# A window-attention block with a routed mixture of experts: the score bias copied into the score banks by ScalarE, with a new order of work on every queue

## What is computed

```python
attn = jnp.einsum('whnd,whmd->whnm', q, k) * scale + bias[None]     # 8x8 windows, 4 heads
attn = jax.nn.softmax(attn, axis=-1)
out = jnp.einsum('whnm,whmd->whnd', attn, v)
...
x = x + _L0_conv_ref(_ln_c(x), ...)        # windowed attention on channel-normalised x
t = t + _L0_ffn_ref(_ln_t(t), ...)         # per token: top 2 of 8 experts, 64x64 each, gated
```

## Time and profile before

| | |
|---|---|
| median of 3 runs | 1152.08 us (1149.42 to 1155.35) |
| profiled execution, span | 1154.0 us |
| TensorE busy | 1050.4 us (91%), mean granted clock 0.985 |
| VectorE busy | 875.0 us (76%) |
| ScalarE busy | 748.4 us (65%) |
| GpSimd busy | 463.1 us (40%) |
| transfers | 189.61 MB, 164 GB/s |

### The profile page before, as it was taken

The page is one execution under the profiler, slowest core; times in us unless marked ns, Lnnn a source line. Parts: engine busy times, 40 slices in busy tenths (PEclk is TensorE's granted clock), DMA queues, the critical chain, the costliest instruction groups (busy, mean ns, idle before and its releaser), DMA issues.

```text
span 1154.0 us, 39247 instructions
## 1 busy us (share of the span) xinstructions
PE 1050.4 (91%) x16886; PEld 597.6 (52%) x16886; DVE 875.0 (76%) x1355; ACT 748.4 (65%) x1218; POOL 463.1 (40%) x509
## 2 busy tenths in 40 slices
PE   4798899999999999999999999999999999988857
PEld 3455555555555555555555544555555555554312
DVE  4567678878777777787777877778887787787874
ACT  1688577767776767677766666777776677665410
POOL 1013443444344334434434443443434434443550
PEclk9999999999999999999999999999999999999878
DMA  6016467878777668877776787677778876747885
GB/s 188 2 39 138 106 148 173 202 184 193 177 168 170 171 166 192 194 172 170 181 168 166 187 187 181 155 177 180 177 176 193 195 172 164 171 112 178 190 179 130
DMA packets 48872, 189.61 MB, mean 164 GB/s; under 512 B 10494, under 2 KB 10750, under 8 KB 32572
## 3 DMA queue, kind: packets, MB, share of 16 engines
q1 hardware_dynamic: 48700, 187.10, 68.3%
HBM read 151.15 MB, written 18.87 MB: 147 GB/s over the span
## 4 chain that ended last, share of the span: by engine, by line
PE 59%; DVE 19%; POOL 7%; DMA 6%; issue 6%; ACT 2%; SPq 0%; POOLq 0%; DVEq 0%; ACTq 0%
PE bank L568 8%; PE bank L689 8%; PE bank L585 8%; PE bank L546 5%; PE bank L559 5%; DMA gz<-gates_dram 5%; DVE Ls L1827 5%; PE bank L602 4%; PE bank L609 4%; DVE probs L1728 3%; DVE mx L1721 3%; PE bank L621 3%; PE bank L516 3%; POOL vr L1527 3%; PE bank L630 2%
## 5 line engine op out<-in xcount | busy, mean ns | idle before, releaser
L689 PE MATMUL bank<-gz,wex 64*64 64x512 f32 x2048 | 259.4, 612 | 9.0 <-DVE gz L1743 9.0
L1536 POOL TENSOR_TENSOR gz<-gz,tt 128x1024 f32<-128x1024 f32 x94 | 229.2, 2440 | 63.9 <-DMA gz<-gates_dram 63.9
L1117 ACT ACTIVATE pt<-bank 128x512 f32<-128x512 f32 x256 | 151.7, 593 | 119.7 <-PE bank L585 118.8
L1728 DVE TENSOR_TENSOR probs<-bank,mx 128x1024 f32<-128x1024 f32 x128 | 156.7, 1224 | 94.7 <-PE bank L585 91.6
L1743 DVE TENSOR_TENSOR gz<-gz,tt 128x1024 f32<-128x1024 f32 x156 | 196.9, 1280 | 5.0 <-DMA gz<-gates_dram 5.0
L1497 POOL TENSOR_TENSOR tt<-prj,xs 128x512 f32<-128x512 f32 x64 | 82.4, 1308 | 291.3 <-ACT prj L1134 291.3
L1721 DVE TENSOR_REDUCE mx<-bank 128x16 f32<-128x1024 f32 x128 | 156.0, 1219 | 34.4 <-PE bank L568 33.5
L585 PE MATMUL bank<-cst,probs 128*128 128x128 f32 x1024 | 165.7, 285 | 3.0 <-ACT pt L1117 2.5
L585 PEld LDWEIGHTS bank<-cst,probs 128*128 128x128 f32 x1024 | 111.7, 141 | 87.8 <-issue 67.5
L568 PE MATMUL bank<-km,qs 32*64 32x128 f32 x4096 | 143.8, 275 | 4.8 <-issue 4.8
L689 PEld LDWEIGHTS bank<-gz,wex 64*64 64x64 f32 x2048 | 74.2, 135 | 125.6 <-issue 104.2
(11 more groups left out here) (122 smaller groups left out, 1480.0 us busy)
## 6 DMA issues: line engine op xcount, KB each, us to landing
gz<-gates_dram SPq DMA_DIRECT2D x250, 512.0 KB, 8.7
xs<-in_x SPq DMA_DIRECT2D x32, 512.0 KB, 9.0
tx<-tt SPq DMA_DIRECT2D x128, 128.0 KB, 2.8
out<-ob SPq DMA_DIRECT2D x128, 128.0 KB, 9.9
gz<-in_rel SPq DMA_DIRECT2D x1, 2048.0 KB, 9.5
gates_dram<-gt_rs SPq DMA_DIRECT2D x32, 64.0 KB
cst<-in_consts SPq DMA_DIRECT2D x1, 359.0 KB, 3.0
tt<-in_weights SPq DMA_DIRECT2D x4, 64.0 KB, 5.0
```

What stands on the lines that cost most here:

```text
L689: last = mm(bank[64 * x:64 * x + 64, Y_BANK + a, :], wex[64 * a:64 * a + 64, e, :], gz[64 * a:64 * a + 64, s.pair(e)[1], e % 2, x * CH:(x ...
L1117: af(pt[g % 2][:, u % 2, :, :, :, :].rearrange("p j h x q -> p (j h x q)"), bank[:, PT_BANK, :], ACT.Copy).then_inc(pt_ready, 1)
L1536: tt_(gz[:, k, e % 2, :], gz[:, k, e % 2, :], tt[s.buf(4)][:, :], op=ALU.mult).then_inc(z_pool, 1)
L1728: tt_(probs[g % 2][:, :, :, :].rearrange("p h w (m k) -> p (h w m) k", k=N), two_banks(S_BANK).rearrange("p (c k) -> p c k", k=N), mx[g % ...
```

## The change

Bias products on TensorE are replaced by a copy on ScalarE, `put_bias`, one per score group: it writes `bias` (float32, now a tile of its own), repeated over windows, into both score banks once `shift` has read the group before; `scores` waits for it and adds all its products on top. `tile_id` and `bias_hl` and the operations that made them are dropped. `open_scores` runs one product per score bank at the start, so that later products add onto what lies in the bank. `bias_rows` gathers into the expert banks instead of the score banks.

```diff
             def scores(s, g):
                 if g == 0:
                     pe.wait_ge(q_ready, s.count(1, 1))
                     pe.wait_ge(k_ready, s.count(2, 2))
-                    if s.c == 0:
-                        pe.wait_ge(bias_ready, 1)
-                wait(pe, shift_done, s.count(GROUPS, g))
-                for hp in range(2):
-                    mm(bank[:, S_BANK + hp, :], tile_id[:, :],
-                       bias_hl[:, 2 * hp:2 * hp + 2, :].rearrange("p h k -> p (h k)").unsqueeze(1).broadcast_to(
-                           [P, 4, 2 * N]), start=True, stop=False, skip_group_check=True)
-
+                pe.wait_ge(bias_put, s.count(GROUPS, g + 1))
...
+            def open_scores():
+                for hp in range(2):
+                    last = mm(bank[:, S_BANK + hp, :], cv("ident"), cst[:, 0:512], start=True, stop=True)
+                last.then_inc(scores_open, 1)
...
+            def put_bias(s, g):
+                if s.c == 0 and g == 0:
+                    act.wait_ge(scores_open, 1)
+                    act.wait_ge(bias_part, 6)
+                wait(act, shift_done, s.count(GROUPS, g))
+                af(two_banks(S_BANK).rearrange("p (h i k) -> p h i k", h=2, k=2 * N),
...
+                   ACT.Copy).then_inc(bias_put, 1)
```

More of the change, by code:

```diff
@@ L387, in _ @@
             spread_gates(strips[0], 3)
+            load(strips[5])
             write_gates(strips[1])
@@ new lines, in _ @@
+            transposes(strips[4], 2)
+            experts(strips[0], 5)
+            project(strips[3])
+            transposes(strips[4], 3)
+            experts(strips[0], 6)
+            queries(strips[5])
+            experts(strips[0], 7)
+            values(strips[4], 0)
+            values(strips[4], 1)
+            denominators(strips[4], 0)
+            channel_sums(strips[6])
+            router(strips[3])
+            transposes(strips[4], 4)
+            transpose_logits(strips[3])
@@ new lines, in _ @@
+            experts(strips[1], 0)
+            keys(strips[5])
+            values(strips[4], 2)
+            values(strips[4], 3)
+            denominators(strips[4], 1)
+            experts(strips[1], 1)
+            scores(strips[5], 0)
+            transposes(strips[4], 5)
+            experts(strips[1], 2)
+            experts(strips[1], 3)
+            transposes(strips[4], 6)
+            spread_std(strips[6])
+            scores(strips[5], 1)
+            transposes(strips[4], 7)
+            values(strips[4], 4)
@@ new lines, in _ @@
+            values(strips[4], 5)
+            denominators(strips[4], 2)
+            expert_bias_rows(strips[1])
+            transposes(strips[5], 0)
+            experts(strips[1], 4)
+            scores(strips[5], 2)
+            transpose_gates(strips[3])
+            transposes(strips[5], 1)
+            values(strips[4], 6)
+            values(strips[4], 7)
+            denominators(strips[4], 3)
+            value_rows(strips[5])
+            scores(strips[5], 3)
+            transposes(strips[5], 2)
@@ new lines, in _ @@
+            channel_sums(strips[-2])
+            router(strips[-5])
+            transposes(strips[-4], 4)
+            transpose_logits(strips[-5])
+            experts(strips[-7], 0)
+            experts(strips[-7], 1)
+            values(strips[-4], 2)
+            values(strips[-4], 3)
+            keys(strips[-3])
+            transposes(strips[-4], 5)
+            denominators(strips[-4], 1)
+            expert_bias_rows(strips[-7])
+            scores(strips[-3], 0)
+            transposes(strips[-4], 6)
@@ new lines, in _ @@
+            variance(strips[-2])
+            gated(strips[-7], 6)
+            move_logits(strips[-5])
+            normalise(strips[-4], 0)
+            guard_variance(strips[-2])
+            logits(strips[-5])
+            top_one(strips[-5])
+            pick_one(strips[-5])
+            top_two(strips[-5])
+            pick_two(strips[-5])
+            row_max(strips[-3], 0)
+            split_std(strips[-2])
+            shift(strips[-3], 0)
+            gates(strips[-5])
+            gated(strips[-6], 0)
```

1139 lines of the change are left out of this document (673 added, 466 removed).

## The result

The changed kernel takes **1093.6 us** (median; 1092.9 to 1095.6) against 1152.2 for the kernel before on the same chip: ratio 0.947, 95% interval 0.944 to 0.950 (the quotient of the two medians is 0.949). The forecast was 1096.0. The profiled execution has a span of 1091.5 us against 1154.0, so 62.5 us have to be accounted for.

What follows compares the result with a forecast made beforehand. TensorE was taken to set the 32.56 us period; 9.1 + 20.3 + 0.75 + 0.45 gave 30.6. Saving 49 us over 25 periods and 7 outside took 1154.0 to 1098 profiled, so 1096 us; own range 1068 to 1122.

Steps and rivals of the forecast that it cites:

- The path through the first part: From T to the start of score group 1: 11.29 us before the change, forecast to fall to 9.1 us.
- T: The moment in each loop period when the transposes of the logits end on TensorE.
- the 1.66 charged: Scaling of the logits, held up by GpSimd's gate product: 1.95 us would fall to 0.29, saving 1.66 us per period.
- The variance step's 0.95 us: Token variance step on GpSimd, held up by VectorE: 1.17 us would fall to 0.22, saving 0.95 us per period.
- The second part: From score group 1 to the next T: 21.94 us would become 20.3, before 0.75 us added for stops.
- 0.75 us for stops of groups 2 and 3: Added per period because maximum, shift and write of score groups 2 and 3 follow the group before, with other steps queued between.
- 0.45 for a full ScalarE: Added per period, 0.45 us, for a ScalarE that is 90% full and served in order.
- The single stops: TensorE stops in the loop that no work releases: 33.23 - 32.56 = 0.67 us a period, forecast to stay unchanged.
- Fill and drain: The 323 us outside the 25 loop periods, seven strips: forecast gain 1 us a strip, 7 us, bounds 0 and 19.
- The hold-up moves: Rival, chance 0.12: GpSimd's later gate product blocks VectorE's, ahead of the logits' move, by up to 2.4 us; about 1155 us.
- ScalarE becomes the bound: Rival, chance 0.12: with 27.5 us of ScalarE work, waits for shifts stop all moves; period 31.6 us, total 1124 us.
- The slow write: Rival, chance 0.09: each us beyond 1.05 per write costs about 4 us a period; at 2.1 us, 1224 us total.

## Why the prediction was right, and where it was not

**The path through the first part: right.** 9.1 us were forecast from T to group 1, 9.21 measured. Scaling (0.29) and variance step (0.22) took their free prices, and the write 1.03 plus 0.05 to the scores for 1.10. One thing was not foreseen: a second path ends at the same moment. The split of the deviations stands behind the same shift on VectorE, TensorE waits 0.23 us for it at 566.09, and the scores follow that product 0.67 us later, at 566.76, when the write has been over for 0.05 us. (With GpSimd's old order they also start 0.67 us after it.) Putting the gate product back in front of the logits lengthened the part by 1.52 us, near the 1.66 charged.

**The variance step's 0.95 us: right for the part, too much for the period.** Holding GpSimd up again cost 0.78 us there and 0.30 in the period, since VectorE's product has to run somewhere.

**The second part and the period: right in the sum, partly by luck.** 30.6 us forecast, 30.59 measured, of which 0.50 are two small "issue" stops. The first (561.71), the wait for the keys, stands in every period. The second (576.29) is a single stop, though a small one: it ends 1.48 us after an instruction packet landed, and a period without it takes 30.1 in the runs above. TensorE's busy time was to fall to 28.8 and is 29.72. A part of that, 10.7 us over 32 strips or 0.33 each, is the experts': 270.1 us for 259.4, with as many records but now spread over the period in more and smaller blocks. The forecast of idle time was too high by about as much: of the 0.75 us for stops of groups 2 and 3 and the 0.45 for a full ScalarE, the rows of this period show no wait for a write and 0.25 us for ScalarE (the keys). So two errors cancel. ScalarE's load was put at 27.5 us and is 26.4; the 27.5 left out that a write overlaps its neighbours.

**The single stops: wrong.** "I leave as they are" is the step that failed. They grew from 33.23 - 32.56 = 0.67 us to 31.39 - 30.59 = 0.80 a period, and measured from the 30.1 of the periods without any, to 1.3. Set against the prediction this costs 24 x 0.13 = 3 us: 24 x 1.96 = 47 us were expected of these periods, 44.3 came.

**Fill and drain: mis-sized.** 7 us and the 25th period's 2 were forecast, 18.2 measured. In the fill nothing is gained (4.9 us lost). The stop of 3.28 us that ends at 113.15, with the granted clock at 0.51 from 111.8 to 118.7 us behind it, accounts for that: the execution that lacks it, of the kernel with store and swap moved, has its fourth T at 174.1 us, against 174.9 before the change. The granted clock is also 0.50 from 20 to 40 us where it was 1.00; why is not settled, but it does not decide, since the new order with the old products has 1.00 there and reaches the first T no sooner, at 85.3. At the end 23.1 us are gained, 18.0 of it by the order alone. In the tail TensorE's one long wait is 4.9 us, for VectorE's last output, where it was 9.0 for a gate product.

**The range.** The forecast's own range, 1068 to 1122, does not follow from its two terms at their ends (periods of 29.6 to 31.5, fill and drain 0 to 19), which give about 1059 to 1126; the measured time lies well inside both.

**The rivals.** *The hold-up moves:* it did not; VectorE's gate product of 556.13 took its 1.22 us, as it starts about where GpSimd's ends (553.85 + 2.39 = 556.24). *ScalarE becomes the bound:* TensorE waits for the write only where it lies on the path; an undisturbed period is 30.1 with ScalarE at 26.5. *The slow write:* its price per us was right in kind (3.1 us for one more write of 1.03, 4 assumed), its condition did not occur.

**What stays open.** That the single stops end with the arrival of TensorE's instructions is shown by the packets: all 18 in the changed kernel and all 18 in the run with the input load earlier end 1.2 to 1.7 us after one has landed. (With the fourth gate load behind the input load only three of ten do; what the other seven wait for, the profile does not name.) That the packet comes late because it waits behind other transfers is argued, not shown, for the trace records when a packet runs and not when it was asked for. For it speak that packets land 7.6 us apart at the median but 10.9 to 13.4 us apart ahead of 14 of the 18 stops, and that the stops go when the traffic is halved, shrink or move when the block of transfers is broken up, and go when the period is slower. Whether an order of the sync queue removes them without making the gates late was not found.

## What to carry to other kernels

Look in the timelines for operations that take several times their free price, and see which other engine's instruction runs beside them: two places in GpSimd's order were worth about as much here as 256 TensorE products (0.969 without the one, 0.968 without the other), though in the old order, where TensorE's own work and its stops set the period, they were worth next to nothing (0.997). Moving work to an engine with idle time pays only if its place in that engine's queue is right: the same writes lost 11% in one placing in the old order, half of it in the fill, and gained 2.2% in the new (0.947 for 0.968). When the bound engine's idle time has no releaser, look at when the packets of its instruction queue land, move or break up the transfers, and check what that makes late.

## What was not expected of the hardware

TensorE's single stops follow the schedule of the DMA queue, and in the changed kernel each ends 1.2 to 1.6 us after a packet of TensorE's instructions has landed. TensorE's time without a releaser is 26.9 us in 700 in the changed kernel, 38.6 with one more load in the block of transfers, 11.6 with half the gate traffic (half of it in single stops, all before 336 us, the rest the short wait for the keys in every period) and 0.6 in a slower period. A stop of 1.7 to 1.9 us can cost as much again: behind two of them, in the run with GpSimd's old order and in the old kernel with its new order, the granted clock was 0.59 and 0.72 for some microseconds, and the period 1.5 to 3.5 us longer than its neighbours. It need not: behind the changed kernel's own stops in the loop, up to 1.78 us, the granted clock stayed at 1.00.
